# Flamingo gated block on one core: more unread products in TensorE's two pauses, and row maxima of |h| taken two blocks at a time

## The reference, cut to what matters

```python
def _act_fake_quant(x, clip_factor):
    scale = jax.nn.sigmoid(clip_factor) * jnp.max(jnp.abs(x)) / QMAX
    return jnp.clip(_ste_round(x / scale), -QMAX - 1.0, QMAX) * scale
...
xq = _act_fake_quant(x, clip_x[0])
gate = jnp.einsum('bsh,ih->bsi', xq, _weight_fake_quant(w_gate))
up = jnp.einsum('bsh,ih->bsi', xq, _weight_fake_quant(w_up))
h = _act_fake_quant(jax.nn.silu(gate) * up, clip_down[0])
return jnp.einsum('bsi,hi->bsh', h, _weight_fake_quant(w_down))
```

## Time and profile before

| | us |
|---|---|
| median of 3 runs | 244.38 |
| lowest, highest | 244.16, 245.97 |
| the profiled execution | 245.42 |
| its span, first to last instruction | 243.8 |
| PE busy | 216.6 (89%) |
| DVE busy | 202.8 (83%) |
| ACT busy | 162.2 (67%) |
| POOL busy | 132.2 (54%) |

### The profile page before, as it was taken

One profiled execution on the slowest core, in us unless ns is written; L12 is line 12 of the kernel. 1 busy time (PEld: TensorE's weight loads), 2 busy tenths in 40 slices (PEclk: granted clock), 3 DMA queues, 4 the chain that ended last, 5 costly groups with the idle time before them and its releaser, 6 DMA issues.

```text
span 243.8 us, 5608 instructions
## 1 busy us (share of the span) xinstructions
PE 216.6 (89%) x1794; PEld 154.0 (63%) x1797; DVE 202.8 (83%) x416; ACT 162.2 (67%) x300; POOL 132.2 (54%) x238
## 2 busy tenths in 40 slices
PE   6799989979988999999999999989985898984990
PEld 6778868858854676667676666666555443333780
DVE  3378988987998998998999999985698279998892
ACT  2355587455696787887777786876637678973940
POOL 8546567533462253659484866827771456431262
PEclk9999999999999999999999999999999599997696
DMA  6879799999736544444535444000000500000197
GB/s 228 264 232 304 223 299 239 257 256 245 206 108 158 132 134 131 118 117 101 116 104 116 121 130 135 1 4 1 0 4 0 215 3 1 0 4 0 11 149 190
DMA packets 30586, 30.82 MB, mean 126 GB/s; under 512 B 3168, under 2 KB 21600, under 8 KB 30560
## 3 DMA queue, kind: packets, MB, share of 16 engines
q1 hardware_dynamic: 27840, 27.74, 40.5%
q0 software_dynamic: 720, 1.31, 3.8%
q10 hardware_dynamic: 2000, 1.44, 1.9%
HBM read 20.65 MB, written 9.70 MB: 124 GB/s over the span
## 4 chain that ended last, share of the span: by engine, by line
PE 51%; DVE 21%; issue 8%; ACT 8%; DMA 4%; POOL 3%; SPq 3%; ACTq 0%; POOLq 0%; DVEq 0%
PE bank_o L1483 12%; PE bank_a L1466 9%; PE bank_b L1452 7%; PE bank_a L1359 6%; PE bank_a L1492 5%; ACT arena L814 4%; DMA qk_parts<-arena 3%; DVE h_max L1237 3%; DVE big L1246 2%; PE bank_b L1641 2%; PE bank_o L1370 2%; DVE v_all L1277 2%; POOL big L496 1%; DVE arena L1271 1%; PE bank_a L1332 1%
## 5 line engine op out<-in xcount | busy, mean ns | idle before, releaser
L961 DVE TENSOR_REDUCE neg_max<-bank_b 128x2 f32<-128x512 f32 x128 | 80.1, 673 | 4.7 <-PE bank_b L1348 3.0
L1466 PE MATMUL bank_a<-big 98*128 98x256 bf16 x256 | 48.9, 273 | 3.9 <-ACT arena L814 2.3
L1452 PE MATMUL bank_b<-big 96*128 96x256 bf16 x224 | 42.7, 272 | 0.3 <-issue 0.3
L814 ACT ACTIVATE arena<-bank_a 128x512 f32<-128x512 f32 x64 | 34.2, 606 | 9.9 <-PE bank_a L1466 9.9
L814 ACT ACTIVATE big<-bank_a 128x512 f32<-128x512 f32 x64 | 33.8, 599 | 9.4 <-PE bank_a L1466 9.2
L1466 PEld LDWEIGHTS bank_a<-big 98*128 98x128 bf16 x256 | 20.9, 97 | 20.4 <-issue 8.1
L1359 PE MATMUL bank_a<-arena,w_t 128*128 128x256 f32 x128 | 30.2, 381 | 1.8 <-DVE resid L966 1.2
L1359 PEld LDWEIGHTS bank_a<-arena,w_t 128*128 128x128 f32 x128 | 23.2, 190 | 5.1 <-issue 2.4
L526 POOL TENSOR_TENSOR arena<-resid,arena 128x512 bf16<-128x512 f32 x16 | 18.3, 1157 | 10.8 <-ACT arena L730 10.7
L1452 PEld LDWEIGHTS bank_b<-big 96*128 96x128 bf16 x224 | 21.3, 97 | 4.2 <-DVE neg_max L961 0.6
L890 ACT ACTIVATE arena<-bank_b,w_scale_x 128x512 f32<-128x512 f32 (+1 forms) x24 | 16.1, 686 | 6.7 <-PE bank_b L1622 2.6
(11 more groups left out here) (185 smaller groups left out, 443.1 us busy)
## 6 DMA issues: line engine op xcount, KB each, us to landing
qk_parts<-arena SPq DMA_DIRECT2D x8, 768.0 KB, 5.1
big<-qk_parts SPq DMA_DIRECT2D x32, 192.0 KB, 3.3
big<-qk_parts SPq DMA_DIRECT2D x32, 128.0 KB, 3.3
x_rows<-in_x SPq DMA_DIRECT2D x8, 256.0 KB, 4.8
big<-qk_parts SPq DMA_DIRECT2D x32, 64.0 KB, 3.4
big<-in_ctx SPq DMA_DIRECT2D x7, 256.0 KB, 5.0
out<-x_rows SPq DMA_DIRECT2D x7, 256.0 KB, 2.7
out<-v_all POOLq DMA_DIRECT2D x5, 256.0 KB, 4.9
```

Of the source, the lines that this page charges most:

```text
L814: act.activation(probabilities(h), ring_bank(b, ("exp", h)).rearrange("p (c s) -> p c s", c=QC), ACT.Exp, scale=SCALE).then_inc(exp_done, 1)
L961: dve.tensor_reduce(neg_max[:, p, :, h], bank.rearrange("p (c s) -> p c s", c=QC), axis=AX.X, op=ALU.max, negate=True).then_inc(max_done, 1)
L1452: done = mm(to, q_st[0:KR, p, h, c * P:(c + 1) * P], k_st[0:KR, p, h], start=True, stop=not masked)
L1466: done = mm(to, k_st[0:KM, p, h, k * P:(k + 1) * P], q_st[0:KM, p, h], start=True, stop=not masked)
```

## The change

There are two edits. The four runs of unread products grow: 32 to 64 and 16 to 28 at the scale of x, 24 to 50 and 12 to 28 at the scale of h (84 to 170 in all). And the maximum of |h| is taken by one instruction over two neighbouring blocks, so that 12 instructions stand in place of 24; the maxima of blocks 4 and 5 of a chunk are taken in the next chunk, behind its first product (for the last chunk at the end). Block 5 has 64 rows; the pair (4, 5) is read over all 128 partitions, of which the upper 64 of block 5 were cleared before.

```diff
             def h_maximum(n, c):
-                r, u = (P if c < IC - 1 else ILAST), n * IC + c
-                if c in POOL_CHUNKS:
-                    dve.wait_ge(pool_h_done, 2 * n + c // 3 + 2)
-                else:
-                    dve.wait_ge(h_done, 4 * n + DVE_CHUNKS.index(c) + 3)
-                chain.then(dve.tensor_reduce(h_max[0:r, tile(u)], h_all[0:r, c, bass.ds(n * CW, CW)], axis=AX.X, op=ALU.max,
+                pool_c, dve_c = ((1, 0), (None, 3), (4, 5))[c // 2]
+                if pool_c:
+                    dve.wait_ge(pool_h_done, 2 * n + pool_c // 3 + 2)
+                dve.wait_ge(h_done, 4 * n + DVE_CHUNKS.index(dve_c) + 3)
+                u = n * IC + c
+                chain.then(dve.tensor_reduce(h_max[:, u:u + 2], h_all[:, c:c + 2, n * CW:(n + 1) * CW], axis=AX.X, op=ALU.max,
                                              apply_absolute_value=True))
 
             def products(n):
 
-                for c, maxima_of in zip(DVE_CHUNKS, ((), (0,), (2, 1), (3,))):
+                for c, maxima_of in zip(DVE_CHUNKS, ((n - 1, 4), None, (n, 0), (n, 2))):
...
-                    for m in maxima_of:
-                        h_maximum(n, m)
-                h_maximum(n, IC - 1)
-                h_maximum(n, 4)
+                    if maxima_of and maxima_of[0] >= 0:
+                        h_maximum(*maxima_of)
 
             for n in range(NCH):
                 products(n)
+            h_maximum(NCH - 1, 4)
...
-                unread(32, bank_b[:, 1, 0:P])
+                unread(64, bank_b[:, 1, 0:P])
                 pe.wait_ge(x2_done, QC * B)
                 pe.wait_ge(amax_part, 1)
                 spread(bank_m[:, 0:P], TMP).then_inc(amax_spread, 1)
-                unread(16, bank_b[:, 1, 0:P])
+                unread(28, bank_b[:, 1, 0:P])
...
-                unread(24, bank_o[:, 0:P])
+                unread(50, bank_o[:, 0:P])
                 pe.wait_ge(amax_part, 2)
                 spread(bank_m[:, 0:P], TMP2).then_inc(amax_spread, 1)
-                unread(12, bank_o[:, 0:P])
+                unread(28, bank_o[:, 0:P])
```

## The result

| | before | changed |
|---|---|---|
| median of 12 runs, us | 244.52 | 243.21 |
| lowest, highest | 243.80, 246.01 | 242.33, 243.62 |
| profiled execution, us | 245.42 | 242.91 |
| its span, us | 243.8 | 241.3 |

The ratio of the times is 0.9949, 95% interval 0.9924 to 0.9974: half a per cent faster, not the 1.4% forecast, and 243.21 lies above the range's upper end of 242.9. The two profiled executions lie 2.51 us apart and the two medians 1.31. So two things have to be explained: what the profiles show differently from the working (3.8 us), and why the median moved less than the profiles.

A forecast was written before the change was run, and what follows sets the result against it. VectorE's gate and up work and TensorE at half clock were taken to share the path. Terms -2.96 - 0.91 + 0.49 - 0.4 = -3.8 us from 245.42 gave 241.6, or 240.6 as median; 241.0 was taken, range 239.8 to 242.9.

The forecast's parts named there:

- Term A: Scale of x to block 5's product of chunk 0: more unread products keep TensorE at full clock, -2.96 us.
- Terms B and C: Paired maxima: three later chunks of gate and up shorter, -0.91 us; longer reductions behind the last product, +0.49 us.
- the ring through GpSimd: Gate and up loop, silu 4 through GpSimd's product and cast to next silu 4: bounds chunks 1 and 2 at 6.29 us.
- Term D: Scale of h: added products delay nothing, a pause of 1.3 us remains and the clock holds.
- Term E: Down: at full clock VectorE's scaling of the second batch starts right behind the conversion, -0.4 us.
- Rival 3: At both scales the unread products don't hold the clock and become a delay: 245.5 us, chance 0.06.
- Rival 4: Each VectorE reduction costs its full duration, so each pair of maxima saves 0.13 us: 240.6 us, chance 0.05.

The follow-up runs named there:

- the maxima alone: Changed kernel with the four old numbers of unread products (32, 16, 24, 12), keeping the paired maxima: 244.12 us, ratio 0.9997 to the kernel before.
- the pause put back: Changed kernel plus one unread VectorE product in down, ahead of scaling batch 1 (241.88 us, ratio 0.9900) or batch 3 (242.41 us, 0.9897).
- four and six batches: Changed kernel with four or six batches, instead of five, added by accumulating DMAs: four 242.50 us (ratio 0.9918), six 243.74 us (0.9970).
- The products at x alone: Changed kernel with the unread products at the scale of h back at 24 and 12: 243.94 us, ratio 0.9971 to the kernel before.
- the early pause: Changed kernel plus one unread VectorE product of 256 columns ahead of the scaling of batch 1 in down: 241.88 us, ratio 0.9900.

## Why the prediction was wrong, point by point

**Term A** (-2.96) holds for the two profiled executions: 12.23 us from spread to block 5's product became 9.36, -2.87. Nothing shows that it holds for the median. The unchanged kernel's second profile has 9.86 there, so in that execution the same products would have saved 0.5. Term A was the gain over one execution in which the fall came late and lay nearly all over gate and up. How often that happens isn't known: of the three profiles with the old products two are dear.

**Terms B and C** (-0.91 and +0.49) measured -0.77 and +0.47, together -0.30; the same in the maxima alone, and -0.33 beside the products. The start-to-start time of a double maximum was 1.13 us, as worked out from the mask's reduction. The Trainium skill (VectorE: DVE Perf Modes, section on the DRAIN you can't avoid), which the prediction holds against this, adds that a next operation that isn't held starts earlier; 2.33 us for two reductions of 1.20 agree with that, so the trace doesn't speak against the page. Chunk 1 took 6.74 and chunk 2 6.03, where I had 6.29 for each. Neither is the ring through GpSimd by itself: from silu 4 to silu 4 it took 6.39 and 6.38 us (195.01, 201.40, 207.78 on ScalarE), 0.1 more than worked out, and what is above and below it comes from when block 5 is multiplied within its chunk. The two misses of +0.45 and -0.26 cancel in part.

**Term D** (0) holds: 1.27 us of pause left, where 1.3 were worked out, and the clock stayed. What this is worth lies between nothing and 0.9 us: without the products at h the median was higher by 0.7 to 0.9, with intervals that overlap.

**Term E** (-0.4) has the wrong sign: +0.5 at the last addition, +0.7 at the end of the span. The scaling came right behind the conversion, as the step has it. What failed is its silent assumption that VectorE's work, coming sooner, would be passed on. Two things stood behind it. The half clock's pause of 0.34 us on VectorE had kept the end of each of GpSimd's DMA issues clear of VectorE's next int8 to bf16 conversion; without it each issue goes from 0.86 to as much as 2.16 us, and the DMA queues, which bound the end, fill later (0.03 busy instead of 0.21 in the first 2 us). And GpSimd, late with its issues, then makes its own additions beside VectorE's (2.21 instead of 0.53). The runs with the pause put back show the first, the run without GpSimd's additions the second, and the same run and those with four and six batches show that the second doesn't reach the end. The products at x alone don't fit so well: their issues weren't held in the profile, and their median is the highest of the kernels that keep the clock at x. That an issue is held when its last part meets a conversion, and not when its first part does, is how the starts and ends fit; it was not tried by itself. The Trainium skill (SBUF — State Buffer, section "Who interferes with whom") says that a cast in a two-port mode holds the port pair that VectorE shares with GpSimd for its whole instruction, and that this starves GpSimd's descriptor generation too; and that a VectorE instruction with two SBUF inputs contends with a GpSimd instruction that reads SBUF. The trace agrees with the second (0.43 to 2.21) and in the main with the first (0.86 to 2.16). It doesn't show whether these conversions run in a two-port mode, and not every overlap holds: in the run with the early pause the issue of 228.10 starts 0.40 us into a conversion and takes 0.87. The page gives no price; but it is the rule that should have made me ask what lies beside the issues once VectorE runs sooner.

**From the profile to the median.** This step cost less than term E, but it made the forecast too low as well. I set the sum against 245.42 and then chose 241.0, between 241.6 (gain as in the profile, less its 1.04 us of offset) and 240.6. The changed kernel's profiled execution took 242.91, 1.3 above 241.6. The gain between the profiles was 2.51 and between the medians 1.31. Of the 1.20 between them 0.90 is the offset of the profile before from the median of its twelve executions (1.04 from that of the three I had), and 0.30 is luck of the other profile, which lies that much under the changed kernel's median. So the offset had to be taken out of the gain in full: with term A measured from one dear execution, the 1.04 most likely belonged to it. Worked that way, with term E at nothing, it would have been 244.38 - (3.38 - 1.04) = 242.0, and with term E as measured 242.7; the median was 243.21. So of the 2.2 us between forecast and result the offset makes 0.6 (241.6 in place of 241.0 with term E at -0.4), term E 1.1 (+0.7 in place of -0.4), and half a microsecond stays open: the medians of the kernel before alone, 243.86 to 244.71, differ by more than that from one comparison to the next. Part of the scatter lies where no edit reaches: the spread of x comes between 186.65 and 188.14 us in the thirteen profiles. The range wasn't carried down rightly either: its low end, with terms A, B and E at their far ends, comes to 239.5, not 239.8.

**The rivals.** None of the four happened. Rival 3, the one on the slower side, had its mechanism refuted: with 64, 28, 50 and 28 identity products the granted clock is 1.00 from 184 us to TensorE's last matmul in all nine profiles of kernels that have them. Rival 4 fails by the 1.13 us of a double maximum, start to start. What happened was a fifth: the reader of VectorE's output, GpSimd, was thrown out of step. I had named the half clock in down as cheap, and had looked only at who waits for VectorE's data and not at who shares something with it.

## What to carry to other kernels

Take a second profile of the same kernel before a gain is read off a stretch at half clock: where the clock falls, and how much of the fall lies in pauses, differed here by a factor of six in worth (2.9 and 0.5 us). When a stall on VectorE goes, look at what GpSimd does in that stretch, its DMA issues too, because a stall can be what keeps the two apart. And when the end of a kernel is full DMA queues, count a gain by when the queues fill and by how many bytes are accumulated rather than stored, not by the last arithmetic instruction.

## What the hardware showed that I had not expected

The clock of TensorE falls at different moments in different executions of one program: at 188.8 or at 186.5, for 6.8 or 3.4 us, with the same pause ahead of the spread (2.37 and 2.42 us). In the one it falls 1.2 us behind the spread, in the other 0.3 us before it.

An accumulating DMA's issue on GpSimd, 0.86 us where nothing holds it, takes 1.55 to 2.16 us beside int8 to bf16 conversions of 128x1536 on VectorE, and falls into step with them: once held, each next one is held too, until 0.42 us of other work on VectorE breaks it.

An addition of 128x256 on VectorE takes 0.43 us alone and 2.21 us beside GpSimd's additions of 128x512; in the kernel before, where the two overlapped as well, it was 0.53 and 1.03.
